# VectorE takes a share of the softmax-denominator sums in the first attention, and the last MLP closes tile by tile in buffers of its own

## What is computed

```python
# first stage: 16 heads of 32, causal
q = concat([q_sem, q_geo]); k = concat([k_sem, k_geo])
scores = where(causal, q @ k.T * scale, -inf)
attn = softmax(scores)
out = (attn @ v) @ Wo.T
x = layernorm(x + out)
...
# last stage: gated MLP with 2:4 sparsity, inner width 2048
h = silu(x @ w_gate) * (x @ w_up)
h = of each group of 4 values the 2 largest in magnitude, the others 0
x = layernorm(x + h @ w_down)
```

## Time and profile before

| | us |
|---|---|
| median of three runs | 2225.41 |
| the profiled execution | 2230.52 |
| its span, first to last instruction | 2228.7 |
| TensorE busy in it | 2130.8 (96%) |
| VectorE, GpSimd, ScalarE busy | 1190.0, 824.5, 736.7 |
| first attention, roughly | 180 to 730 |
| last MLP, roughly | 1674 to 2228.7 |

### The profile page before, as it was taken

The page is one execution under the profiler, slowest core; times in us unless marked ns, Lnnn a source line. Parts: engine busy times, 40 slices in busy tenths (PEclk is TensorE's granted clock), DMA queues, the critical chain, the costliest instruction groups (busy, mean ns, idle before and its releaser), DMA issues. The chain is left out here.

```text
span 2228.7 us, 27156 instructions
## 1 busy us (share of the span) xinstructions
PE 2130.8 (96%) x9788; PEld 1456.9 (65%) x9788; DVE 1190.0 (53%) x2306; ACT 736.7 (33%) x1264; POOL 824.5 (37%) x527
## 2 busy tenths in 40 slices
PE   7999999999997999999989999999999999999997
PEld 6875444444442654444467878888877888888886
DVE  5787777777762653222256633223246545564666
ACT  3324555555555322111144422111123211221123
POOL 4354889988999114432222340000003011212100
PEclk9988999999999999999999999999999999999999
DMA  5578355343310626555444360000101010100001
GB/s 180 182 199 191 93 125 139 96 96 72 72 32 18 252 101 230 131 99 92 79 146 141 133 217 29 19 19 29 38 1 57 1 38 20 38 19 28 10 19 57
DMA packets 104604, 197.24 MB, mean 89 GB/s; under 512 B 10384, under 2 KB 27664, under 8 KB 103056
## 3 DMA queue, kind: packets, MB, share of 16 engines
q1 hardware_dynamic: 92064, 162.78, 24.9%
q0 software_dynamic: 11408, 29.69, 5.9%
q10 hardware_dynamic: 1008, 3.15, 0.4%
HBM read 123.82 MB, written 71.75 MB: 88 GB/s over the span
## 5 line engine op out<-in xcount | busy, mean ns | idle before, releaser
L752 ACT ACTIVATE a_probs<-a_stb 128x512 f32<-128x512 f32 (+1 forms) x449 | 241.6, 587 | 189.8 <-PE a_stb L898 93.6
L2306 POOL CAST m_wh<-wst 128x1024 fp32r<-128x1024 f32 x24 | 26.6, 1108 | 719.4 <-POOLq L1591 369.2
L711 POOL TENSOR_TENSOR a_probs<-a_probs 128x1024 f32<-128x1024 f32 (+3 forms) x138 | 266.9, 1960 | 51.2 <-PE a_avb L914 35.7
L789 DVE TENSOR_REDUCE a_mparts<-a_sbank 128x1 f32<-128x512 f32 x384 | 240.4, 683 | 71.8 <-PE a_sbank L866 71.2
L57 PE MATMUL m_gu<-hi,m_wh 128*128 128x512 f32 x512 | 199.8, 390 | 3.0 <-DVE m_h L2436 1.6
L59 PE MATMUL m_gu<-hi,m_wl 128*128 128x512 f32 x512 | 199.4, 389 | 0.0
L58 PE MATMUL m_gu<-lo,m_wh 128*128 128x512 f32 x512 | 199.3, 389 | 0.0
L2385 DVE TENSOR_TENSOR m_h<-m_sg,m_gu 128x512 f32<-128x512 f32 x63 | 43.3, 687 | 191.6 <-ACT m_sg L2336 191.3
L794 DVE CUSTOM_DVE_ANT_0 a_junk<-a_sbank,hidden 128x128 bf16<-128x128 f32 (+3 forms) x256 | 113.7, 488 | 48.8 <-PE a_sbank L866 47.4
L866 PE MATMUL a_sbank<-hi,q 96*128 96x512 f32 (+3 forms) x320 | 121.5, 405 | 7.9 <-DVE a_mparts L789 3.2
L2336 ACT ACTIVATE m_sg<-m_gu 128x512 f32<-128x512 f32 x64 | 38.3, 598 | 261.3 <-PE m_gu L59 261.2
(11 more groups left out here) (324 smaller groups left out, 4943.9 us busy)
## 6 DMA issues: line engine op xcount, KB each, us to landing
hi<-qk SPq DMA_DIRECT2D x66, 256.0 KB, 5.2
qk<-v_hl SPq DMA_DIRECT2D x32, 512.0 KB, 2.9
lo<-qk SPq DMA_DIRECT2D x54, 256.0 KB, 5.2
wst<-in_w_mlp SPq DMA_DIRECT2D x24, 512.0 KB, 3.5
q<-qk SPq DMA_DIRECT2D x42, 256.0 KB, 6.4
xs<-a_zeros POOLq DMA_DIRECT2D x39, 264.0 KB, 3.0
X<-xs SPq DMA_DIRECT2D x39, 264.0 KB, 2.7
v<-vhl SPq DMA_DIRECT2D x16, 512.0 KB, 4.0
```

Source lines behind the costliest of these rows:

```text
L711: nc.gpsimd.tensor_tensor(probs[to % PSLOTS][:, hs, w0:], probs[to % PSLOTS][:, hs, w0:], probs[other % PSLOTS][:, hs, w0:], ALU.add)\
L752: nc.scalar.activation(to, got, ACT.Exp, scale=SCALE0).then_inc(s["exp_ok"], 1)
L789: nc.vector.reduce_max(to, sbank[:, b, :], AX).then_inc(s["unit_max"], 1)
```

## The change

In the first attention the sums of a block are dealt out by half and by engine. From c = 1 on, VectorE makes the second half of A; in the last item VectorE makes both halves of A and of C, and GpSimd only B. The sum stands in VectorE's list after the scores of step b+2, head 2 (C: step b+5, head 2). One semaphore for sums becomes two, one per engine. In the closing of the last MLP the chunk picked in halves gets buffers of its own for the high and low parts, on top of weights that are no longer read; GpSimd makes the first half's low part; chunk 3 is added, normed and stored tile by tile.

```diff
 def sums_plan(items, steps, first, final):
+    def add(to, other, after, engines, at=None):
+        for half, engine in enumerate(engines):
+            count[engine] += 1
+            halves[len(adds), half] = (engine, count[engine])
+        adds.append((to, other, after))
+        if "dve" in engines:
+            beside.setdefault(at, []).append(len(adds) - 1)
     for n, (c, g) in enumerate(items):
+        alone = n == len(items) - 1
...
             if c == 0:
-                adds += [(b, b + 1, b)]
+                add(b, b + 1, b, ("pool", "pool"))
...
             elif end < len(steps) - 1:
-                adds += [(b, b + 1, b), (b + 2, b, b + 2), (b + 2, b + 3, b + 2)]
+                add(b, b + 1, b, ("dve", "dve") if alone else ("pool", "dve"), (b + 2, 2))
+                add(b + 2, b, b + 2, ("pool", "pool"))
+                add(b + 2, b + 3, b + 2, ("dve", "dve") if alone else ("pool", "pool"), (b + 5, 2))
...
             else:
-                adds += [(b, b + 1, b)]
+                add(b, b + 1, b, ("dve", "dve"), (b + 2, 2))
 def attention0_plan():
...
             order.append(("scores", i, h))
+            order += [("sum", at) for at in beside.get((i, h), [])]
             order += in_gap[k]
 def layer0_attention(...):
         @block.gpsimd
...
-                        for a in range(2):
-                            hs = slice(2 * a, 2 * a + 2)
+                        for half in range(2):
+                            if halves[at, half][0] != "pool":
+                                continue
                             if other > to:
-                                pool.wait_ge(s["exp_ok"], group[other, 2 * a + 1][0] + 1)
-                            if a == 0:
-                                pool.wait_ge(s["av_ok"], i + 1)
-                            if at > 0:
-                                pool.wait_ge(s["sum_ok"], 2 * at + a - 1)
+                                pool.wait_ge(s["exp_ok"], group[other, 2 * half + 1][0] + 1)
+                            pool.wait_ge(s["av_ok"], i + 1)
+                            if adds[at - 1][0] in (to, other):
+                                wait_sum(pool, at - 1, half)
+                            sum_of(nc.gpsimd, at, half).then_inc(s["pool_sum"], 1)
         @block.scalar
...
-                        act.wait_ge(s["sum_ok"], 2 * added[old] + h // 2 + 1)
+                        for half in range((h + 1 - per) // 2, h // 2 + 1):
+                            wait_sum(act, added[old], half)
         @block.vector
...
+                elif ev[0] == "sum":
+                    to, other, after = adds[ev[1]]
+                    for half in range(2):
+                        if halves[ev[1], half][0] != "dve":
+                            continue
+                        if other > to:
+                            dve.wait_ge(s["exp_ok"], group[other, 2 * half + 1][0] + 1)
+                        dve.wait_ge(s["av_ok"], after + 1)
+                        if adds[ev[1] - 1][0] in (to, other):
+                            wait_sum(dve, ev[1] - 1, half)
+                        sum_of(nc.vector, ev[1], half).then_inc(s["dve_sum"], 1)
         @block.tensor
...
-                    pe.wait_ge(s["sum_ok"], 2 * den_of["adds"])
+                    for half in range(2):
+                        wait_sum(pe, den_of["adds"] - 1, half)
 def layer1_mlp(...):
+        last_hh, last_hl = (b[:, 0:2, :].rearrange("p i (a n) -> p (i a) n", a=2) for b in (wh, wl))
...
-                   ("down", c, q, 0), ("finish", c - 1, q, (0, TC))]
-            for i in range(2):
-                ev += [("half add", c, q, i), ("finish", c, q, (2 * i, 2 * i + 2))]
-            return ev
+                   ("half low", c, q, 1), ("down", c, q, 0), ("moments", c - 1, q, (0, TC)), ("shift", c - 1, q, (0, TC))]
+            for t in range(TC):
+                ev += [("tile add", c, q, t), ("moments", c, q, (t, t + 1))]
+                ev += [("shift", c, q, (t - 1, t))] * (t > 0)
+            return ev + [("shift", c, q, (TC - 1, TC))]
         @block.gpsimd
...
+            half = slice(0, CH // 2)
+            for r in range(4):
+                pool.wait_ge(s["hh_ok"], 4 * (NQ * NC - 1) + r + 1)
+                nc.gpsimd.tensor_tensor(last_hl[:, r, half], h[:, r, half], f32(last_hh[:, r, half]), ALU.subtract)\
+                    .then_inc(s["last_hl_ok"], 1)
         @block.scalar
...
-                        if not start:
+                        if what == "pick" and not start:
                             act.wait_ge(s["y_ok"], i * TC)
+                        high = hh if what == "pick" else last_hh
...
-                            nc.scalar.activation(hh[:, r, cols], h[:, r, cols], ACT.Copy).then_inc(s["hh_ok"], 1)
+                            nc.scalar.activation(high[:, r, cols], h[:, r, cols], ACT.Copy).then_inc(s["hh_ok"], 1)
         @block.vector
...
+                    elif what == "half low":
+                        cols, p = slice(r * CH // 2, (r + 1) * CH // 2), i + r
+                        for r in range(4):
+                            dve.wait_ge(s["hh_ok"], 4 * p + r + 1)
+                            tt(last_hl[:, r, cols], h[:, r, cols], f32(last_hh[:, r, cols]), ALU.subtract)\
+                                .then_inc(s["hl_ok"], 1)
...
-                        for r in range(4):
+                        for r in range(4) if what == "pick" else ():
                             dve.wait_ge(s["hh_ok"], 4 * p + r + 1)
                             tt(hl[:, r, cols], h[:, r, cols], f32(hh[:, r, cols]), ALU.subtract)\
         @block.tensor
...
-                        pe.wait_ge(s["hl_ok"], (i + 1) * 4)
...
+                        if last_one:
+                            pe.wait_ge(s["last_hl_ok"], 4)
+                        else:
+                            pe.wait_ge(s["hl_ok"], (i + 1) * 4)
+                        high, low = (last_hh, last_hl) if last_one else (hh, hl)
...
                             if last_one and t == TC // 2:
-                                pe.wait_ge(s["hl_ok"], (i + 2) * 4)
+                                pe.wait_ge(s["hl_ok"], (i + 1) * 4)
```

More of the change, by code:

```diff
@@ L563, in attention0_plan @@
     order = list(before)
-    dens = sums_plan(items, steps, first, final)[1]
+    _, dens, _, _, beside = sums_plan(items, steps, first, final)
     k = 0
@@ L596, in layer0_attention, with wait_sum, sum_of @@
     group, groups_to = score_groups(items, steps)
-    adds, dens, added = sums_plan(items, steps, first, final)
+    adds, dens, added, halves, beside = sums_plan(items, steps, first, final)
     read_by = {i: d for d, den in enumerate(dens) for i in den["reads"]}
+    def wait_sum(eng, at, half):
+        engine, value = halves[at, half]
+        eng.wait_ge(s["pool_sum" if engine == "pool" else "dve_sum"], value)
+    def sum_of(nc_engine, at, half):
+        to, other, _ = adds[at]
+        n, kt = steps[max(to, other)]
+        w0, hs = max(0, kt - TC * items[n][0]) * P, slice(2 * half, 2 * half + 2)
+        return nc_engine.tensor_tensor(probs[to % PSLOTS][:, hs, w0:], probs[to % PSLOTS][:, hs, w0:],
+                                       probs[other % PSLOTS][:, hs, w0:], ALU.add)
     with ExitStack() as ctx:
@@ L2340, in run @@
                         nc.scalar.activation(a[:, :, cols], h[:, :, cols], ACT.Abs).then_inc(s["a_ok"], 1)
[L2341 removed]
+                        if what == "pick" and not start:
                             act.wait_ge(s["y_ok"], i * TC)
+                        high = hh if what == "pick" else last_hh
                         for r in range(4):
                             act.wait_ge(s["hs_ok"], p * 4 + r + 1)
[L2345 to L2346 removed]
+                            nc.scalar.activation(high[:, r, cols], h[:, r, cols], ACT.Copy).then_inc(s["hh_ok"], 1)
+                    elif what == "moments":
+                        for t in range(*r):
+                            nrm.root(act, c * TC + t, NT + c * TC + t)
+                    elif what == "shift":
                         tiles = [c * TC + k for k in range(*r)]
[L2348 to L2349 removed]
                         act.wait_ge(s["minus_ok"], tiles[-1] - (NC - 2) * TC + 1)
@@ L2385, in run @@
                         tt(h[:, r, :], sg[:], gu[:, r % 2, 1, :], ALU.mult).then_inc(s["h_ok"], 1)
-                    elif what in ("add", "half add"):
-                        for t in range(TC) if what == "add" else range(2 * r, 2 * r + 2):
+                    elif what in ("add", "half add", "tile add"):
+                        these = {"add": range(TC), "half add": range(2 * r, 2 * r + 2), "tile add": range(r, r + 1)}[what]
+                        for t in these:
                             dve.wait_ge(s["y_ok"], i * TC + t + 1)
```

31 lines of the change are left out of this document (12 added, 19 removed).

## The result

The changed kernel takes 2248.15 us (median of four runs, 2243.1 to 2257.8) against 2225.14 for the kernel before on the same chip: 1.010 times as long, with a 95% interval of 1.0062 to 1.0137. It is slower by about 23 us. The forecast was 2218.4, with a range to 2234.0. The profiled execution took 2243.1 us (span 2241.2), the shortest of its four, and that of before 2230.52, above its median; so the two traces show 12.5 us of the 23.

A forecast was written before the change was run, and what follows sets the result against it. TensorE, busy 96% of the span, was taken as the bound. -5.6 + 3 - 4.3 = -6.9, rounded to -7, from 2225.4 gave 2218.4 us; the range ran from just below 2206 to 2234.

The forecast's parts named there:

- Part 1: First attention's last item: sums moved to VectorE let exponentials and denominators come earlier; -5.6 us, between -3 and -9.
- the waits of the earlier trace: TensorE's waits around the last item, 3.85 and 1.49 us for exponentials, 1.50 and 1.69 for sums; each to fall under 1.5.
- The rival that the last item does not gain: Last item: the two engines only alternate, so moving sums gains 0 there, giving 2224 us; chance 0.17.
- Part 2: Other eleven items: 6.8 us of new TensorE stalls less 3.7 us of steady waits removed; +3 us, between -4 and +24.
- VectorE got in at that end: First attention, at 691.70: VectorE enters when GpSimd's current instruction ends, so it waits at most 2.34 us, mean 1.17.
- The row that I set aside: VectorE piece at 675.11 took 8.62 us, entering only after GpSimd's run of five sums; taken as evidence for slower behaviour.
- the two rows that I preferred: VectorE instructions at 691.70 (1.59 us) and 1282.5 (1.70 us), read as waiting for one GpSimd instruction at most.
- Up to 2.3 us is free: Items 4 to 14: VectorE may be away 2.3 us without TensorE waiting, read from each item's reciprocal (2.8 away, 0.46 wait).
- Slower: Items 4 to 14: GpSimd keeps the SBUF port through a run of sums; +24 us there, 2239 us in all; chance 0.15.
- Part 3: Last layer's closing: own buffers remove VectorE's 4.05 us idle, GpSimd's turns costing 0.6; -4.3 us, between -2.1 and -5.3.

The follow-up runs named there:

- the last item alone: Kernel before, plus VectorE making sums in the last item only, old closing and items 4 to 14 unchanged: 2224.51 us, ratio 0.9993; run again 2222.85 us.
- the kernel with the wait: New sum shares with the old closing, GpSimd starting its half of A only after VectorE's half, against the kernel before: 2221.11 us, ratio 0.9968.
- the one wait that takes away the failed step: Whole change plus GpSimd starting its half of A only after VectorE's half, against the kernel before: 2217.35 us, ratio 0.9965.
- the kernel with the later place: New sum shares with the old closing, VectorE's half of A in items 4 to 14 three heads later, against the kernel before: 2231.19 us, ratio 1.0030.

## Why the prediction was wrong

**Part 1 (the last item, -5.6): the size was right in the stage, not in the time.** In its own stretch it measured -5.5 us. Not every step was right: of the waits of the earlier trace rows, those for sums (1.50, 1.69) are gone, and 3.85 is 0.94, but 1.49 became 2.24, since B's second half ends as long behind the item's multiplication as before (6.7 us, 6.6 before), and the wait of 1.45 at the item's start stays (1.54). What the part lacked is a term behind the attention: on the mean of the profiles 2.8 us are given back there, mostly at the lower clock, and in the time the last item alone is not to be told from no change. The rival that the last item does not gain was wrong by its mechanism, that the engines only alternate. The Trainium skill's warning in Perfetto Trace Analysis, "Optimizing Scalar/DVE Operations", that moving work between these two engines may not help, held for the other items, with the 22.5 us of part 2.

**Part 2 (items 4 to 14, +3): the step that failed.** The measured price is 22.5 us. Two things went wrong in it. The first is "VectorE got in at that end", with GpSimd's state at VectorE's asking spread evenly, so that no absence passes 3.56 us. The average was right, and that is luck: the 21 full halves took 2.29 us, against 2.2. But they fall into two groups. Fourteen took 1.21 to 1.91 us and seven 3.58 to 5.15: in these VectorE's half came up during a sum of GpSimd behind which the next was ready, and the next went first. TensorE's waits for the maxima grew by 15.0 us (7.8 to 22.8), where the part had 6.8. The row that I set aside, 8.62 us, was of this stage; four of GpSimd's sums, not five, ended while it waited. Of the two rows that I preferred one was of another stage, but 691.70 was of this one, so the rows did not settle it. The Trainium skill's rule in SBUF — State Buffer, "SBUF: two separate sides", that the pair is held for one instruction, sets how long one holder keeps it but not who is next; by my reading of it the wait would end with C, 0.43 us later, and the trace shows 2.8 (563.27 to 566.08).

The second is that the part had no term for the clock. "Up to 2.3 us is free" was read from a reciprocal that stood alone. In an item's first block it now stands right behind a sum of 3.65 us. Of the 8.0 us that an item takes longer than in the kernel with the wait (61.96 against 53.91), about 5, an estimate, are the 10.2 us at half the clock, and some 2.6 are waits for the maxima (10.8 against 3.1 us over items 12 to 14). The rival *Slower* had the first mechanism, GpSimd going on with the next A ahead of VectorE, and its price for this part, +24, is near the 22.5; but that is partly luck, since it took a stall of 1.26 us in each of 21 blocks and no clock, while the first blocks of a few late items carry nearly all. It was given 0.15 on the ground that one row spoke for it and two against.

**Part 3 (the closing, -4.3): right.** 4.2 and 4.3 us in two profiles, -4.7 by the runs. The pause of 4.05 us went, TensorE's last product followed without a gap (at 2218.63; it waits 1.26 us in its middle, for the second half's low part), and GpSimd's turns cost 0.55 us at 2213.81 and 0.43 at 2217.23, 1.0 in all against the 0.6 taken.

With the one wait that takes away the failed step, the whole change measured 2217.4 us; the sum of the prediction was 2218.4. That they are so near is luck. In the time the last item alone brings some 1.6 us and not 5.6, and with the wait items 4 to 14 show no cost where the sum had +3: -7.1 us by the ratio against -1.6 for the last item alone, and with the new closing -7.8 against -6.5.

## What to carry to other kernels

When two engines that exclude each other share one operation, look at the moment at which the second one's turn comes and at what the first has ready then, not at idle shares or average lengths: here one wait on the engine with time to spare was worth 26 us. Price a wait of TensorE together with what stands next to it: here two waits of 2.8 us in all were followed by 10 us at half the clock, some 5 us more. And check that a gain at the end of one stage arrives at the end of the program, since the clock of the next stage can take it back.

## What the runs showed of the hardware

- In items 4 to 14 of the changed kernel GpSimd's next two-input sum, where it was ready, went ahead of VectorE's half-sum that was already waiting (0.43 us of one and 2.38 of the next at 563.27): seven times out of seven, at the same seven halves in three profiles. It is not always so, in this stage neither. In the kernel before, VectorE's piece at 691.70 got in between two of GpSimd's sums, and it was GpSimd's second that grew, 2.26 us against 1.80 for the equal one behind it:

```profile
692.71 2.26 POOL L711 TENSOR_TENSOR a_probs<-a_probs 128x768 f32<-128x768 f32 x1
694.93 1.80 POOL L711 TENSOR_TENSOR a_probs<-a_probs 128x768 f32<-128x768 f32 x1
```

  The same at 1282.5 us of that kernel, in another stage, with GpSimd's from 1.30 to 1.74 us (VectorE's row, then GpSimd's):

```profile
1282.52 1.70 DVE L1939 TENSOR_TENSOR q_turned<-q_turned,q_across 128x512 f32<-128x512 f32 x1 [1.18 <-POOL q_turned L1723]
```

```profile
1282.38 1.30 POOL L1740 TENSOR_TENSOR X<-X,bv 128x512 f32<-128x512 f32 x1
1283.63 1.74 POOL L1740 TENSOR_TENSOR X<-X,bv 128x512 f32<-128x512 f32 x1
```

  What decides between the two was not settled.
- A VectorE maximum with one input from the same buffers runs at 1.21 us beside a GpSimd that is busy without a pause.
- Two waits of TensorE of 1.29 to 1.42 and 1.43 to 1.49 us close together came with low clock (0.50, for 3.4 to 10.2 us) at the starts of items 11 to 14 in all three profiles with these waits, twelve times out of twelve. Single waits of 1.36 to 1.40 us inside items 12 and 13 of the same three profiles were followed by none, six times out of six, and a single one of 0.76 us at the start of item 13, in the kernel with GpSimd's wait, was not either. But without VectorE's half in the first blocks one of two single waits of 1.38 us was followed by 3.4 us, in the kernel with the later place waits of 0.27 and 0.88 us by 3.4 and 6.8, and the pause of 1.94 us in the routing by 10.2 us in nine of eleven profiles, where one of 2.30 us was by none in three. So the length of one pause does not decide it alone.
